# Masked CB kept in PSUM, softplus and the pick's steps laid among other VectorE work

## The reference, cut to what matters

```python
h = qw[input]                      # rows of a table rounded to 8 bits per row
h = h + attn(layernorm(h))         # "attn" is a state-space block
h = h + ffn(layernorm(h))          # two sets of four experts

# attn, for every chunk of 128 tokens (here one sequence)
zxbcdt = feature @ in_proj_w.T
dt = softplus(zxbcdt[..., -NHEADS:] + dt_bias)
xBC = silu(conv over 4 tokens of xBC + conv_b)
A_cum = cumsum(dt * A);  Lmat = exp(segsum(dt * A))     # lower triangle
CB = einsum('bcln,bcsn->bcls', C, B)
Y = einsum('bcls,bhcls,bcshp->bclhp', CB, Lmat, x * dt) + D * x
y = Y * silu(z);  y = y * rsqrt(mean(y * y) + EPS) * norm_w
return sigmoid(gate1) * (y @ out_proj_w.T) + feature

# ffn: softmax router of 4 experts twice ("common", "unique")
route = argmax(softmax(h @ Ws + bs))
common = expert(h, route_c); unique = expert(h, route_u)
out = common + dropped * unique    # dropped: beyond a capacity, by the router's probability
```

## Time and profile before

| | us |
|---|---|
| median of 3 runs | 1054.59 |
| profiled execution | 1053.83 |
| its span, first to last instruction | 1052.1 |
| TensorE busy | 922.6 (88%) |
| VectorE busy | 680.2 (65%) |
| ScalarE busy | 567.9 (54%) |
| GpSimd busy | 576.4 (55%) |

### The profile page before, as it was taken

The page is one execution under the profiler, slowest core; times in us unless marked ns, Lnnn a source line. Parts: engine busy times, 40 slices in busy tenths (PEclk is TensorE's granted clock), DMA queues, the critical chain, the costliest instruction groups (busy, mean ns, idle before and its releaser), DMA issues.

```text
span 1052.1 us, 20009 instructions
## 1 busy us (share of the span) xinstructions
PE 922.6 (88%) x5764; PEld 600.3 (57%) x5765; DVE 680.2 (65%) x2004; ACT 567.9 (54%) x1163; POOL 576.4 (55%) x751
## 2 busy tenths in 40 slices
PE   2787989898888898988988979899999999999986
PEld 2233554455455554554545767677776767677764
DVE  3678999899899998998989633666661121212220
ACT  2658876887788767877776243232323333323320
POOL 7424635556656466565542457334337777775552
PEclk9879999999999999999999798999999999999997
DMA  4920010011101110110000212224332221223220
GB/s 94 324 63 16 16 46 31 18 46 47 35 15 47 46 36 13 46 48 32 3 32 31 63 51 84 58 80 150 99 94 56 56 67 50 67 53 86 62 59 19
DMA packets 50147, 61.54 MB, mean 58 GB/s; under 512 B 22668, under 2 KB 41832, under 8 KB 49556
## 3 DMA queue, kind: packets, MB, share of 16 engines
q0 software_dynamic: 16704, 30.54, 10.2%
q1 hardware_dynamic: 28724, 24.91, 8.0%
q10 hardware_dynamic: 4640, 5.13, 1.7%
HBM read 36.22 MB, written 25.92 MB: 59 GB/s over the span
## 4 chain that ended last, share of the span: by engine, by line
PE 42%; DVE 28%; ACT 12%; issue 11%; POOL 3%; DMA 1%; DVEq 0%; ACTq 0%; POOLq 0%
DVE xbc L1481 10%; PE cx L1267 6%; PE yb L1267 6%; PE mm L1255 5%; PE mm L1251 5%; PE mm L1121 4%; PE sg L1251 4%; PE mm L1125 3%; DVE mix L1501 3%; DVE ybuf L1514 2%; PE tp L1088 2%; DVE st L1364 2%; ACT rows_s L805 2%; ACT h L752 2%; ACT ht L953 1%
## 5 line engine op out<-in xcount | busy, mean ns | idle before, releaser
L1481 DVE SCALAR_TENSOR_TENSOR xbc<-mm,cw,xbc 128x508 f32<-128x508 f32 (+2 forms) x231 | 168.4, 740 | 24.0 <-ACT xbc L780 18.6
L1121 PE MATMUL mm<-xt_a,win_a 128*128 128x512 f32 x248 | 145.4, 670 | 36.5 <-DVE xbc L1481 27.1
L953 ACT ACTIVATE ht<-mm,b1s 128x256 f32<-128x256 f32 x102 | 44.6, 471 | 226.0 <-PE sg L1255 223.4
L648 POOL DMA_INDIRECT xg<-hr_dram,ids x80 | 80.7, 1009 | 86.9 <-DVE res L1820 44.5
L780 ACT ACTIVATE xbc<-mm,cb,cw 128x512 f32<-128x512 f32 x77 | 56.5, 774 | 119.2 <-PE mm L1125 119.2
L667 POOL DMA_INDIRECT out_dram<-osb,ids_s x80 | 82.4, 1030 | 63.9 <-DVE osb L1830 44.4
L531 POOL TENSOR_TENSOR ybuf<-ybuf,zs 128x384 f32<-128x384 f32 x64 | 72.3, 1130 | 72.3 <-DVE ybuf L1514 70.0
L1830 DVE TENSOR_TENSOR osb<-cx,res 128x192 f32<-128x192 f32 x40 | 14.2, 356 | 134.9 <-PE cx L1267 133.2
L1251 PE MATMUL mm<-fx_a,w1a_t 128*128 128x256 f32 x240 | 82.5, 426 | 9.8 <-issue 7.7
L1255 PE MATMUL mm<-fx_b,w1b_t 64*128 64x256 f32 x240 | 86.1, 440 | 0.0
L1255 PE MATMUL sg<-fx_b,w1b_t 64*128 64x256 f32 x240 | 86.1, 440 | 0.0
(11 more groups left out here) (295 smaller groups left out, 2073.4 us busy)
## 6 DMA issues: line engine op xcount, KB each, us to landing
hr_dram<-hr SPq DMA_DIRECT2D x16, 768.0 KB, 3.6
w2s<-in_w2c_dram SPq DMA_DIRECT2D x4, 576.0 KB
w2s_u<-in_w2u_dram ACTq DMA_DIRECT2D x4, 576.0 KB
list_c<-fill SPq DMA_DIRECT2D x2, 1032.0 KB, 12.7
list_u<-fill SPq DMA_DIRECT2D x2, 1032.0 KB, 18.8
w1a<-in_w1c_dram SPq DMA_DIRECT2D x4, 384.0 KB
w1a_u<-in_w1u_dram ACTq DMA_DIRECT2D x4, 384.0 KB
xg<-hr_dram,ids POOLq DMA_INDIRECT x80, 3.1
```

Of the source, the lines that this page charges most:

```text
L648: nc.gpsimd.indirect_dma_start(out=xg[:, v, t, :], out_offset=None, in_=rows, in_offset=bass.IndirectOffsetOnAxis(ap=ids[:, v, t, 0:1], ax ...
L1121: mmul(tile_bank(g2, m)[:, :], win_a[:, column(m):column(m) + P], xt_a[:, p, :], start=True, stop=False)
L1481: ins = stt(out=dst_[:, :, back:L], in0=src[:, :, 0:L - back], scalar=cw[:, m, TAPS - 1 - back:TAPS - back], in1=dst_[:, :, back:L], op0=A ...
```

## The change

The masked CB is written back over CB in its PSUM bank and read from there by the mix; `cbm` goes. TensorE waits for the mix before it refills the bank. `more` and `acc` go: the running counts have a row of their own in `oh`, before or behind the batch's rows, and `places` makes the next batch's by one sum over the batch's rows and that row. `Chain` gets `go` (issue and count) and `join` (wait), so that work can stand between; softplus is cut into its steps, laid among the taps of `conv(4)`, the residual and the tiles of y(2); the steps of `pick` have the statistics of the second norm between them. The two copies of one-hots stand further ahead, and `s_oh` goes up with the first.

```diff
+    def go(self, ins):
+        self.n += 1
+        ins.then_inc(self.sem, 1)
+
+    def join(self):
+        self.eng.wait_ge(self.sem, self.base + self.n)
+
...
-        cbm = sb("cbm", [P, P], c=a)
...
+        oh = sb("oh", [P, 2 * GS + 2, 2, NE], c=a)
+
+        def picked(b, n):
+
+            o = 1 if b % 2 == 0 else 1 + 2 * GS - n
+            return oh[:, o:o + n, :, :]
+
+        def running(b):
+
+            return oh[:, 0 if b % 2 == 0 else 2 * GS + 1, 0, :]
+
+        def with_running(b, n):
+
+            return (oh[:, 0:n + 1, 0, :] if b % 2 == 0 else oh[:, 1 + 2 * GS - n:2 * GS + 2, 0, :]).rearrange("p j e -> p e j")
...
-                    wait(pe, s_xd, GS * g3 + j)
+                    wait(pe, s_m, GS * g3 + j)
...
+                def soft_sum():
+                    if g2 is not None:
+                        dve.wait_ge(s_u, g2 + 1)
+                        soft.go(ts(S1, U, 2.0, None, ALU.add))
+
+                def soft_inverse():
+                    if g2 is not None:
+                        soft.join()
+                        soft.go(v.reciprocal(S2, S1))
...
+                def soft_term(k):
+                    if g2 is not None:
+                        soft.join()
+                        soft.go(stt(out=S3, in0=S3, scalar=SERIES[k], in1=S1 if k == 0 else S2, op0=ALU.add, op1=ALU.mult))
+
+                def soft_steps():
+                    if g2 is not None:
+                        soft.join()
+                        stt(out=dts[:, q, :, :], in0=sd[:, slot, :, DTR:DTR + HEADS], scalar=0.0, in1=S3,
+                            op0=ALU.max, op1=ALU.add).then_inc(s_dts, 1)
+                        soft.end()
...
-                            link(ins)
+                            link.go(ins)
+                            beside[back - 1]()
+                            link.join()
...
-                    wait(dve, s_m, GS * g3 + j)
-                    link(tt(cbm[:, :], cx[:, 0:P], le[:, :], ALU.mult))
+                    link.go(tt(cx[:, 0:P], cx[:, 0:P], le[:, :], ALU.mult))
                     wait(dve, s_yp, GS * g3 + j - 1)
                     tt(xd[:, j % 2, :].rearrange("p (h n) -> p h n", h=HEADS),
                        cx[:, P:4 * P].rearrange("p (h n) -> p h n", h=HEADS),
                        dts[:, p, j, :].unsqueeze(2).broadcast_to([P, HEADS, HD]), ALU.mult).then_inc(s_xd, 1)
+                    link.join()
                     dve.wait_ge(s_e, GS * g3 + j + 1)
                     stt(out=mix[:, j % 2, :, :], in0=dec[:, j % 2, :, :], scalar=1.0,
-                        in1=cbm[:, :].unsqueeze(1).broadcast_to([P, HEADS, P]), op0=ALU.min, op1=ALU.mult).then_inc(s_m, 1)
-
-                def y(j):
+                        in1=cx[:, 0:P].unsqueeze(1).broadcast_to([P, HEADS, P]), op0=ALU.min, op1=ALU.mult).then_inc(s_m, 1)
...
+                def rows_read():
+                    if g4 is not None:
+                        dve.wait_ge(s_h1, 2 * g4 + 2)
+                        wait(dve, s_xn2, g4)
+
+                def row_moments(j):
+                    if g4 is not None:
+                        ins = v.bn_stats(st2[:, j, :], hr[:, g4 % 2, j, 0:D])
+                        if j == GS - 1:
+                            chains["h1"].go(ins)
+
+                def row_sums():
+                    if g4 is None:
+                        return
+                    chains["h1"].join()
+                    for j in range(GS):
+                        last = v.bn_aggr(mv2[:, j, :], st2[:, j, :])
+                    chains["h1"].go(last)
+
+                def row_shift():
+                    if g4 is None:
+                        return
+                    chains["h1"].join()
+                    ts(var2[:, :], mv2[:, :, 1], LNEPS, None, ALU.add)
+                    ts(minus2[:, :], mv2[:, :, 0], -1.0, None, ALU.mult).then_inc(s_ve2, 1)
...
-                    link(v.tensor_reduce(e8[:, 0:n5, :], el[:, 0:n5, :, :], AX.X, ALU.max))
+                    link.go(v.tensor_reduce(e8[:, 0:n5, :], el[:, 0:n5, :, :], AX.X, ALU.max))
                     v.tensor_reduce(s8[:, 0:n5, :], el[:, 0:n5, :, :], AX.X, ALU.add)
-
-                    link(tt(r8(pk), r8(el), b8(e8), ALU.is_equal))
-                    link(tt(r8(pk), r8(pk), w4[:, :].unsqueeze(1).broadcast_to([P, n5 * 2, NE]), ALU.mult))
-                    link(v.tensor_reduce(m8[:, 0:n5, :], pk[:, 0:n5, :, :], AX.X, ALU.max))
-                    link(tt(r8(oh), r8(pk), b8(m8), ALU.is_equal))
-                    v.tensor_reduce(more[:, :], oh[:, 0:n5, 0, :].rearrange("p j e -> p e j"), AX.X, ALU.add).then_inc(s_oh, 1)
-                    link(v.reciprocal(s8[:, 0:n5, :], s8[:, 0:n5, :]))
+                    beside[0]()
+                    link.join()
+
+                    link.go(tt(r8(pk), r8(el), b8(e8), ALU.is_equal))
+                    beside[1]()
+                    link.join()
+                    link.go(tt(r8(pk), r8(pk), w4[:, :].unsqueeze(1).broadcast_to([P, n5 * 2, NE]), ALU.mult))
+                    beside[2]()
+                    link.join()
+                    link.go(v.tensor_reduce(m8[:, 0:n5, :], pk[:, 0:n5, :, :], AX.X, ALU.max))
+                    beside[3]()
+                    link.join()
+                    oh_ = picked(b5, n5)
+                    link.go(tt(oh_.rearrange("p j r e -> p (j r) e"), r8(pk), b8(m8), ALU.is_equal))
+                    beside[4]()
+                    link.join()
+                    v.tensor_copy(ohc[:, at, :], oh_[:, :, 0, :]).then_inc(s_oh, 1)
+                    link.go(v.reciprocal(s8[:, 0:n5, :], s8[:, 0:n5, :]))
+                    v.tensor_copy(ohu[:, at, :], oh_[:, :, 1, :])
+                    beside[5]()
+                    link.join()
                     tt(conf[:, at], s8[:, 0:n5, 0], e8[:, 0:n5, 0], ALU.mult)
-                    v.tensor_copy(ohc[:, at, :], oh[:, 0:n5, 0, :])
-                    v.tensor_copy(ohu[:, at, :], oh[:, 0:n5, 1, :])
...
-                    tt(acc[:, :], acc[:, :], more[:, :], ALU.add)
+                    v.tensor_reduce(running(b + 1), with_running(b, n), AX.X, ALU.add)
...
-                conv(4)
-                residual(0)
-                softplus()
-                y(2)
+                conv(4, (soft_sum, soft_inverse))
+                soft_ratio()
+                residual(0, (0,))
+                soft_square()
+                residual(0, (1,))
+                soft_top()
+                y(2, (0,))
+                soft_term(3)
+                y(2, (1,))
+                soft_term(2)
+                y(2, (2,))
+                soft_term(1)
+                soft_term(0)
+                soft_steps()
+                soft_rates()
 
                 weights(3)
                 residual(1)
-                pick()
-                stats2()
+                rows_read()
+                pick((lambda: row_moments(0), lambda: row_moments(1), lambda: row_moments(2), lambda: row_moments(3),
+                      row_sums, row_shift))
```

More of the change, by code:

```diff
@@ L484, in _ @@
             for e in range(NE):
-                last = nc.gpsimd.memset(acc[:, e:e + 1], float(e * LIST // P))
+                last = nc.gpsimd.memset(oh[:, 0, 0, e:e + 1], float(e * LIST // P))
             for s_ in (s_oh, s_el, s_dest, s_d, *s_st):
@@ L1319, in _ @@
             out_product(1)
-            pe.wait_ge(s_xd, GS * NG)
+            pe.wait_ge(s_m, GS * NG)
             pe.wait_ge(s_yd, GS * NG)
@@ new lines, in soft_ratio, with soft_square, soft_top @@
+                def soft_ratio():
+                    if g2 is not None:
+                        soft.join()
+                        soft.go(tt(S1, S2, U, ALU.mult))
+                def soft_square():
+                    if g2 is not None:
+                        soft.join()
+                        soft.go(tt(S2, S1, S1, ALU.mult))
+                def soft_top():
+                    if g2 is not None:
+                        soft.join()
+                        soft.go(ts(S3, S2, SERIES[-1], None, ALU.mult))
@@ L1444, in softplus, with soft_rates @@
+                def soft_rates():
                     if g2 is None:
                         return
[L1446 to L1460, removed]
@@ L1471, in softplus, with nothing, conv @@
                     last.then_inc(s_dt, 1)
-                def conv(m):
+                def nothing():
+                    pass
+                def conv(m, beside=(nothing, nothing)):
                     if g2 is None:
@@ L1508, in y, with residual @@
                     p, js = g3 % 2, slice(j * L, (j + 1) * L)
-                    if j == 0:
-                        wait(dve, s_o, 2 * (g3 - 1))
-                    dve.wait_ge(s_yp, GS * g3 + j + 1)
-                    for c in range(ZT):
+                    if tiles[0] == 0:
+                        if j == 0:
+                            wait(dve, s_o, 2 * (g3 - 1))
+                        dve.wait_ge(s_yp, GS * g3 + j + 1)
+                    for c in tiles:
```

(25 more changed lines are left out.)

26 lines of the change are left out of this document (16 added, 10 removed).

## The result

The changed kernel takes 1041.01 us (median of 4 runs, 1038.71 to 1045.53), the kernel before beside it 1054.82 (4 runs, 1050.86 to 1056.61): ratio 0.9884, 95% interval 0.9842 to 0.9925. The profiled execution takes 1042.34 (span 1040.3) where that of before takes 1053.83: 11.5 us less. The forecast was 1042.5 (1036 to 1049), 12.2 us less.

A forecast was written before the change was run, and what follows sets the result against it. VectorE was taken to bound stage A's even turns, the mixed loop the odd ones. Even 9.4 + odd 2.5 + last turn 0.3 = 12.2 us off 1053.83: 1041.6; median 0.76 higher: 1042.5 (1036 to 1049).

The forecast's parts named there:

- What bounds a turn: Stage A: even turn bound by VectorE at 35.0 us, odd turn by the mixed loop at 33.88.
- the mixed loop: Stage A loop through ScalarE's gapless 15.03 us, TensorE's sums and projections, and VectorE's convs; 33.38 us in the even turn.
- VectorE's saving behind `conv(2)`: Even turn, conv(2) to next conv(0): VectorE 3.2 us less, of which 1.6 reaches the end.
- A wait: Each wait between VectorE instructions costs 0.12 us, read from starts of conv taps.
- The rival of free waits: VectorE's waits cost nothing, only blocked mix and count are won: 7.4 us, 1047; chance 0.08.
- Masked CB in PSUM: Mix reads masked CB from PSUM at 0.01 us, taken as nothing; xd's dropped wait saves 0.48 a turn.
- The rival of a slow mix: Mix reading PSUM at a third of the rate takes 1.6 us more each: 26 us slower, 1081; chance 0.04.
- Running counts: Odd turn, gap before conv(2): the reduce replacing the 0.84 us add takes 0.13, so 0.63 less.
- TensorE 0.12 late in the odd turn: Odd turn: TensorE's projection for conv(1)'s bank ends 0.12 us late, leaving 0.41 won of 0.53.
- y(3): Odd turn's second half: VectorE waits 0.4 us for TensorE before y(3), at no cost.
- The last turn: Stage A's last turn: TensorE's 0.31 us wait ahead of CB(1) goes, 0.3 us won.
- TensorE takes it back: Third rival: seven more clock falls in the mixed loop cost 11 us: 1053, no change; chance 0.07.

The follow-up runs named there:

- The order alone: Kernel before with only TensorE's seg(3) and transposes ahead of out_product(0), ScalarE's with_rest ahead of start(4), decays(3) ahead of from_tp(0): 1118.4 us, one run.
- the order on top: Changed kernel with TensorE's seg(3) and transposes ahead of out_product(0), ScalarE's with_rest ahead of start(4), decays(3) ahead of from_tp(0): 1100.19 us; again 1102.26 us, ratio 0.9757.
- both in one piece again: Changed kernel with softplus in one piece and the pick ahead of the statistics again, two of the pick's waits still covered: 1040.45 us.
- the kernel with softplus laid: Kernel before with softplus laid among taps, residual and y(2), two of the pick's waits also covered: 1052.12 us, one run.
- ScalarE's part alone: Changed kernel with ScalarE's with_rest (four copies) moved ahead of start(4), TensorE's order unchanged: 1106.88 us, one run.

## Why the prediction was right, point by point

- *What bounds a turn.* Right. 33.39 for the 33.38 worked out from the mixed loop, ScalarE's stretch unchanged, and VectorE idle before `conv(0)`. The order alone (35.03) and the order on top (32.47) show both loops from their own side.
- *VectorE's saving behind `conv(2)`.* 3.2 said. By the idle time in brackets: before 373.50 − 346.08 = 27.42; after 368.18 − 342.38 − 1.75 idle = 24.05; 3.37 less. By starts it is some 3.5, since an instruction that follows without a wait starts some 0.08 before the one ahead of it ends, and the two brackets leave that out. Its parts, by starts, before and after: `conv(4)` to the masked CB behind it 6.40 and 5.28, 1.12 less (softplus, 1.05 said); `residual(1)` to y(3) 4.44 and 3.34, 1.10 less (pick with `more`, 0.96 said); the three weights 1.2 (0.36 + 0.82 said); and 0.12 ahead of the router's first reduce, which I had not counted and whose cause is open. With both in one piece again these stretches take 6.44 and 4.11, so 0.33 of the 1.10 is `more` and the two covered waits.
- *A wait.* Taps around a laid step start 384.49, 385.27 and 386.13, so 0.78 and 0.86 apart, as said. The rival of free waits is out: with free waits, softplus in one piece would not have moved VectorE's idle time by 1.07, from 1.75 to 0.68.
- *Masked CB in PSUM.* The mix's median fell from 950 to 944 ns where I allowed +10; none is held up. That xd's fell from 557 to 546 goes with the wait that is gone, not with the place of the CB: it is 547 with the CB back in SBUF, and 557 with the CB in PSUM behind its wait. The rival of a slow mix is out.
- *Running counts.* The step that failed. The reduce itself takes 0.22 us, not 0.84, as its single SBUF input said, but the odd turn won 0.18 where 0.41 was forecast. GpSimd's gate still runs from 373.64 to 374.63, and the cast behind the reduce now waits it out: 0.70 us instead of the 0.16 it took behind the add. The gate after, and the cast before:

```profile
373.64 0.99 POOL L550 TENSOR_TENSOR ybuf<-ybuf,zs 128x384 f32<-128x384 f32 x1 [4.54 <-DVE ybuf L1563]
```

```profile
310.99 0.16 DVE L1597 CAST desti<-dest 128x8 int32<-128x8 f32 x1
```

  It is so every time: the six casts of stage A that start while a gate runs take 634 to 766 ns, the three outside one 148 to 162. The gap before `conv(2)` became 3.61 − 0.20 = 3.41, not 2.86. I had priced the instruction and not the place: the first blocked instruction shields those behind it. The Trainium skill has a rule for it: by "SBUF — State Buffer" (SBUF: two separate sides) an instruction with two SBUF inputs and one in a two-port mode stand under the same exclusive lock with GpSimd, and by "VectorE: DVE Perf Modes" (The perf-mode tier table) an fp32 copy within SBUF runs in such a mode and a reduce never does. The cast's 703 against 160 ns and the reduce's 0.22 us agree with both, if a cast counts as the copy of that table, which names none.
- *TensorE 0.12 late in the odd turn.* Not seen in the changed kernel: its four matmuls of projections 2 and 3 run on without a bracket from 371.64, and from `conv(2)` to `conv(0)` the odd turn has 25.78 us as before. With places ahead of y(0), where the gap does fall to 3.09, that stretch is 0.15 longer.
- *y(3)* waits 0.48 us for TensorE in turn 11 (0.4 said) and 0.56 in most other odd turns, y(2) only in turn 15 (0.22), and neither costs anything in the turns shown.
- *The last turn.* 0.3 us said for the transition. TensorE's CB(1) comes at 572.47 without the wait of 0.31 us in the earlier trace rows, as said; but counted from the last `conv(0)` the last mix starts at 49.33 for 49.19, so nothing of it reaches there.
- *The sum.* Without falls of the clock the six even turns would have given 9.3 us (9.4 said) and the odd ones 1.1 (2.5 said), 10.4 for 11.9. The falls took 3.2 of it. The shorter slow stretch in turn 1 gave 2.45 and what follows the last `conv(0)` 3.0, neither of them forecast nor shown to be the change's, and the first `conv(0)` came 0.9 later. So that the total is 11.5 for 12.2 is in part luck. (The forecast adds 0.76 to 1041.6, which is 1042.4, not 1042.5.)
- *TensorE takes it back*, the third rival, happened in part, but not by more falls: there are five before and five after, and all five after cost 0.9 to 1.6 us where three before cost nothing. Those three begin 1.1 to 1.8 us into their turn, the two in odd turns after 2.5 and 2.8 us into it; whether the place decides is not tested. In the kernel with softplus laid the falls and their lengths left nothing of the gain (1052.12 against 1050.85, one run each).

## What to carry to other kernels

When several edits shorten the same engine, take each out of the finished kernel and read whether its idle time or its end moves: here the edits saved 3.5 us an even turn, 1.6 landed, and either softplus and pick or the masked CB could be taken out at no cost. Then work on the loop that is left, with all its engines at once: ScalarE's part alone gave nothing, ScalarE's and TensorE's together 0.9 us a turn. And an instruction freed of a held port hands the wait to the next one that uses it, so either the port's other user or all of the instructions beside it must move.

## What the runs showed of the hardware

- A VectorE cast of 128x8 from fp32 to int32 in SBUF takes 0.16 us alone and 0.70 beside GpSimd's gate, a product of two 128x384 tiles in SBUF. A reduce of one SBUF input beside the same gate takes 0.22.
- The holding up goes both ways: a gate that starts while a mix of two SBUF inputs runs takes 1.6 to 1.8 us instead of 1.0 (12 of 64 before), and none more than 1.24 with the mix's second input in PSUM.
- A mix of 128x768 is 944 ns in the median with its repeated input in PSUM, 950 in SBUF, and its longest 956 against 1661.
- A stretch of 3.4 us at 1.2 GHz costs from nothing (turns 5 and 11 before) to 1.65 us (turns 6 and 12 before).
- The same program is 7% longer on another chip, with a ratio to its predecessor that is the same (0.9887 and 0.9884).
